# The rotary tables of a local-attention layer, scaled on GpSimd instead of VectorE from the second layer on

## What is computed

```python
q = l2norm(q) * qs          # qs, ksc: 64 numbers of this layer
k = l2norm(k) * ksc
q = q * cos * scale + rotate_half(q) * sin * scale
k = k * cos * inv + rotate_half(k) * sin * inv
out = local_attention(q, k, v)      # windows of 32 tokens, each sees itself and the one before
return out.transpose(0, 2, 1, 3).reshape(b, n, INNER) @ Wo
```

## Time and profile before

| | |
|---|---|
| median of 3 runs | 4389.28 us (4378.42 to 4394.66) |
| the profiled execution, its own time | 4373.36 us |
| span of the profiled execution | 4371.3 us |
| PE busy | 4046.5 us (93%) |
| DVE busy | 3383.3 us (77%) |
| POOL busy | 2912.9 us (67%) |
| ACT busy | 2584.3 us (59%) |
| products of `factors`, DVE L1143 | 48 instructions, 56.3 us |

### The profile page before, as it was taken

How to read it: one execution, slowest core, us unless ns; L and a number is a source line. 1 busy time by engine, 2 the same in 40 slices (tenths; PEclk the granted TensorE clock), 3 DMA queues, 4 the chain that set the end, 5 groups by cost and what they waited for, 6 DMA issues and landing times. The chain is left out here.

```text
span 4371.3 us, 151568 instructions
## 1 busy us (share of the span) xinstructions
PE 4046.5 (93%) x66856; PEld 2974.8 (68%) x66856; DVE 3383.3 (77%) x4037; ACT 2584.3 (59%) x3022; POOL 2912.9 (67%) x3425
## 2 busy tenths in 40 slices
PE   8989969999999999999868887799999999999997
PEld 5655557777877777877633333677777877777775
DVE  5636568888888888888568884788888888887884
ACT  4424436666666666666437774466666666666664
POOL 2202168887888888888534440788878888888883
PEclk9999989999999999999969997899999999999998
DMA  4304233333233232232100000323332233333221
GB/s 149 123 10 152 94 92 81 86 83 82 70 81 87 81 81 81 73 89 76 32 11 1 1 1 2 107 77 86 81 81 81 73 91 82 81 83 82 74 67 36
DMA packets 164542, 316.94 MB, mean 73 GB/s; under 512 B 38760, under 2 KB 42480, under 8 KB 156848
## 3 DMA queue, kind: packets, MB, share of 16 engines
q1 hardware_dynamic: 153520, 241.18, 20.5%
q0 software_dynamic: 10368, 66.06, 4.7%
HBM read 92.03 MB, written 20.05 MB: 26 GB/s over the span
## 5 line engine op out<-in xcount | busy, mean ns | idle before, releaser
L678 PE MATMUL psum<-loc_w_hl,loc_z_lo 128*128 128x512 f32 x1152 | 514.9, 447 | 33.1 <-DMA loc_w_hl<-parted 26.2
L1079 POOL TENSOR_TENSOR loc_prob<-loc_prob,loc_recip 128x1024 f32<-128x1024 f32 x192 | 365.6, 1904 | 183.0 <-DVE loc_recip L1201 181.6
L924 ACT ACTIVATE loc_sq<-psum 128x1024 f32<-128x1024 f32 x192 | 196.6, 1024 | 468.5 <-PE psum L680 463.5
L1061 POOL TENSOR_TENSOR loc_rc_k<-loc_rc_k,loc_rs_k 128x1024 f32<-128x1024 f32 x192 | 454.0, 2365 | 22.2 <-DVE loc_rs_k L1178 22.2
L1164 DVE TENSOR_REDUCE loc_ssq<-loc_sq 128x16 f32<-128x1024 f32 x384 | 463.8, 1208 | 3.7 <-POOL loc_rn L1057 3.6
L679 PE MATMUL psum<-loc_w_hl,loc_z_hi 128*128 128x512 f32 x1152 | 460.9, 400 | 2.2 <-issue 2.2
L680 PE MATMUL psum<-loc_w_hl,loc_z_hi 128*128 128x512 f32 x1152 | 460.5, 400 | 0.7 <-issue 0.7
L1061 POOL TENSOR_TENSOR loc_rc_q<-loc_rc_q,loc_rs_q 128x1024 f32<-128x1024 f32 x192 | 459.5, 2393 | 0.0
L775 PE MATMUL psum<-loc_PT,loc_V 64*64 64x32 f32 x24576 | 408.8, 221 | 17.5 <-issue 16.8
L775 PEld LDWEIGHTS psum<-loc_PT,loc_V 64*64 64x64 f32 x24576 | 384.9, 136 | 43.4 <-issue 19.9
L795 PEld LDWEIGHTS psum<-loc_outT,loc_wo 128*128 128x128 f32 x3072 | 378.1, 194 | 19.1 <-issue 2.5
(11 more groups left out here) (198 smaller groups left out, 9716.6 us busy)
## 6 DMA issues: line engine op xcount, KB each, us to landing
loc_V<-loc_V SPq DMA_DIRECT2D x1152, 128.0 KB
loc_V<-loc_V SPq DMA_DIRECT2D x672, 64.0 KB
loc_w_hl<-parted POOLq DMA_DIRECT2D x36, 1024.0 KB, 8.2
parted<-moe_halves POOLq DMA_DIRECT2D x18, 1024.0 KB, 5.2
moe_spread<-moe_gates SPq DMA_DIRECT2D x64, 256.0 KB, 4.1
moe_raw<-in_wqkv POOLq DMA_DIRECT2D x18, 512.0 KB, 5.9
moe_w<-in_moe_w SPq DMA_DIRECT2D x32, 256.0 KB, 3.2
loc_wo<-in_wo SPq DMA_DIRECT2D x12, 512.0 KB, 4.1
```

The source lines that it names most:

```text
L678: pe.matmul(M.bank[bank + g], z_lo[:, r, tokens], w_hl[:, k, 0, cols], start=True, stop=False)
L1061: pool.tensor_tensor(rc, rc, rs[:, :], ALU.add).then_inc(added, 1)
L1079: pool.tensor_tensor(both, both, spread_heads(recip[:, :], 2 * WINDOW), ALU.mult).then_inc(p_ready, 1)
```

## The change

DVE makes the four products of `factors` only for the first layer of each local transformer, in the order 2, 3, 0, 1. For layers 2 to 6 POOL makes them: the keys' pair at the end of step 15 of the layer before, after POOL's last addition of rotated keys, and the queries' pair in step 0, after the last queries of the layer before are scaled. DVE waits for the keys' pair ahead of its first product of keys, and for the queries' pair ahead of its first product of queries. Nothing else is moved.

```diff
@@ POOL
+            def factors(L, first):
+                if first == 2:
+                    pool.wait_ge(scales_loaded, L * 16 + 16)
+                for a in range(first, first + 2):
+                    pool.tensor_tensor(rot[:, a, :, :], M.tables[:, a, :, :],
+                                       scales[:, a, :].rearrange("p (o d) -> p o d", o=1).broadcast_to([P, TILES, DH]),
+                                       ALU.mult).then_inc(tables_ready, 1)
...
                     scaled(L, n - 1, q_added, tq_full, rc_q[:, :], 0, qk_q, q_ready)
+                if n == 0 and 0 < L < DEPTH:
+                    factors(L, 0)
...
                     total_of(L, n, k_rotated, rc_k[:, n % 2, :], rs_k, k_added)
+                if n == TS - 1 and L + 1 < DEPTH:
+                    factors(L + 1, 2)
@@ DVE
-            def factors(L):
+            def factors():
-                dve.wait_ge(scales_loaded, L * 16 + 16)
-                for a in range(4):
+                dve.wait_ge(scales_loaded, 16)
+                for a in (2, 3, 0, 1):
...
-                dve.wait_ge(tables_ready, L * 4 + 4)
...
+                    if n == 0 and L == 0:
+                        factors()
                     if n == 0:
-                        factors(L)
+                        dve.wait_ge(tables_ready, L * 4 + 2)
                     by_cosine(L, n, 2, k_squared, X_, rc_k[:, n % 2, :], k_ready, 2)
...
+                    if n == 0:
+                        dve.wait_ge(tables_ready, L * 4 + 4)
                     by_cosine(L, n, 0, q_squared, W_, rc_q[:, :], q_ready, 1)
```

## The result

Seven runs of the changed kernel gave a median of 4359.8 us (4348.68 to 4365.65), seven of the kernel before 4392.15 us (4378.4 to 4399.66). The ratio is 0.9935, with a 95% interval of 0.9913 to 0.9958: 0.65% faster, 28 us, where 10.6 us and "no change that can be told" had been forecast. The direction was right, and so was one of the two terms; the size was not. The time stands at the lower edge of the stated range, 4360 us: 4359.8 us as measured, 4360.8 us when the ratio is applied to the 4389.28 us from which the forecast was made. The profiled execution of the changed kernel took 4365.65 us. The profiled one of before, 4373.36 us, was faster than any of its seven runs, so the two spans differ by 8 us only.

The account below looks back on a forecast made before the run. The prediction took PE to be the bound nearly everywhere, with DVE holding it up only at L808. Terms of -7.2 and -3.4 us made -10.6 us, from 4389.3 to 4378.7 us; range 4360 to 4400 us.

Parts of the forecast that it names:

- The waits at L808: Term one: PE's waits for DVE at L808, over ten layer boundaries of both local transformers, vanish: -7.2 us.
- The low clock behind them: Term two: two stretches at 1.2 GHz behind the waits of 2.48 and 3.0 us at L808 vanish: -3.4 us.
- The queries' pair in POOL's idle time: POOL makes the queries' pair in its wait ahead of `normalise`, 7.24 us before and 3.48 us after: cost nothing.
- The load of the queries' weights: Keys' pair delays this load on POOL by 1.46 us against 1.48 us of slack at the tightest boundary: cost nothing.
- PE's issue waits stay near 30 us: Expected sign: PE's "issue" waits, 31.0 us in layers 2 to 6 of the first local transformer, stay near 30 us.
- PE has no idle time at the boundary of layers 3 and 4: Argument against DVE as pace: PE busy 16.05 of 16.05 us there, from first product of tile 0 to tile 1.
- An earlier DVE has nobody to serve: At the boundary of layers 3 and 4 PE passes L808 without a wait, so freeing DVE gains nothing there.
- Two of the prediction's own signs of being wrong: Step into a new layer 3 us or more shorter where PE had no wait; PE found waiting for queries' weights.
- a third or fourth wait of this kind: Reason for the range's low end, 4360 us: other executions may hold further waits of this kind, some 18 us below 4378.7.
- Nothing is gained: Rival, chance 0.26: PE arrives last at L808 at every boundary, so the moved products free nobody: 4389.3 us.
- All of DVE's time comes back: Rival, chance 0.11: DVE is the true pace of every boundary, so 51.3 us go: 4338.0 us.
- The weights come late: Rival, chance 0.06: keys' pair delays queries' weights past 1.48 us of slack; at 4.73 us a pair, 4421 us.

## Why the prediction came out as it did

**The waits at L808, -7.2 us: right.** They went to zero in the changed kernel and in every kernel that took the keys' pair off DVE, and the two windows with the long waits are shorter by 2.4 and 2.5 us.

**The low clock behind them, -3.4 us: wrong in its place.** At both boundaries for which it was reckoned the low stretch of 3.4 us is still there, behind a wait for instructions instead of the wait at L808. The clock did recover at the three boundaries that became fast, from 0.91 to 1.00, where the prediction had counted nothing.

**The price of a product on POOL, 729 ns: right,** 728 ns.

**The queries' pair in POOL's idle time, cost nothing: not quite.** At the boundary of layers 2 and 3 it was hidden as reckoned. At the three boundaries that became fast, DVE came to it first, and its first product of queries waited for POOL, 1.0 to 1.3 us. This is DVE's timeline at the boundary of layers 3 and 4:

```profile
1362.81 1.23 DVE L1170 TENSOR_TENSOR loc_rc_q<-psum,loc_rot 128x1024 f32<-128x1024 f32 x1 [1.29 <-POOL loc_rot L1085]
```

One step on, PE waits up to 0.7 us for POOL's scaled queries. The experiments with that pair on DVE were no faster.

**The load of the queries' weights, "I put the cost at nothing": the step that failed.** I asked only whether the weights would still land in time, and they did but for 0.7 us in sum. I didn't ask what the moved load had stood in front of. In the kernel before, at three boundaries, the next 16 KB of instructions came only some 6 us behind its issue, when PE had run dry; with the load 1.2 to 2.0 us later they came in time.

That the place of the load decides is shown. At these three boundaries all thirteen traces fall into two groups. In the five kernels with the load at its old place or earlier, issued at most 10.6 us behind DVE's first product of keys of tile 15, the packet starts at 14.9 to 18.0 us, and PE waits 0.9 to 4.0 us for instructions each time. In the eight with the load 11.2 us or more behind it, the packet starts at 12.3 to 14.6 us, and no wait for instructions is over 0.5 us. Both groups hold kernels with the products on DVE and kernels without, so DVE's earliness isn't what removes these waits. How the load holds the packet up inside the DMA engines no run here shows. At the other seven boundaries the changed kernel still waits for instructions, 2.4 to 5.2 us at each.

So "PE's issue waits stay near 30 us" was true of the whole (33.2 us in the two largest rows, after the 31.0 us of the earlier trace rows) and wrong at these three boundaries. "PE has no idle time at the boundary of layers 3 and 4" overlooked the 2.32 us in the earlier trace rows, and the products did not cost DVE most there: 6.36 us for the four of L1143, against 6.69 us at the boundary of layers 2 and 3 of the second transformer, where PE did wait. "An earlier DVE has nobody to serve" was wrong as well: it serves as soon as PE is no longer late. Two of the prediction's own signs of being wrong came true: the step into the new layer took 15.7 us there instead of 21.9 us, and PE was found waiting for the queries' weights, 0.46 and 0.25 us. A third expectation missed: POOL's idle time ahead of `normalise` stayed at 2.7 to 4.1 us at three boundaries.

The worth of it is the step from 0.9978 to 0.9942, 16 us, or some 10 us from the kernel that left the products out. The intervals of either pair overlap; that the later load helps when DVE is free rests on the run with the early and the run with the late load, whose intervals don't. DVE held or free, these are 0 and -10 us with the early load, +8 and -25 us with the late one.

That the time came out at the edge of the stated range is luck. The lower end was set for "a third or fourth wait of this kind", and no such wait was found; the forecast's own range, 4368 to 4389 us, was missed.

**The rivals.** "Nothing is gained" supposed that PE's instruction waits might fall so that an early DVE frees nobody. They did fall differently, but so that it freed PE at more boundaries. "All of DVE's time comes back", 51 us, is refuted: with every product left out the gain was 16 us (7 to 25). "The weights come late" met a pair of 1.41 us and no wait for weights beyond 0.5 us.

## What to carry to other kernels

When an edit shifts a large DMA, even by 1 us, look up in the DMA view which instruction packets fall under it, and count the bound engine's "issue" waits on either side; they are part of the price. So is the low clock behind such a wait: when one wait goes and another stays just ahead of it, the clock may not come back. Where two engines arrive at a meeting point almost together, as PE and DVE do here, relieving one is worth little (10 us, or a loss) and relieving both is worth more than the sum (25 us): judge such edits in pairs, because the late load alone looked like a loss of 8 to 16 us. And for work that isn't urgent, the place in the queue matters more than the engine's rate: GpSimd takes 1.8 times as long for a product as VectorE at its best, and the kernel still gained.

## What the hardware showed that was not expected

The same 1 MB load takes 9.4 us from issue to landing where it is issued 10.5 us behind the first product of keys of tile 15, and 5.5 us where it is issued at 15.7 us. In the earlier place it follows the load of the values' weights, also 1 MB, by 4.9 us. In the run with the earlier load, issued 0.65 us behind that of the values' weights, it took 9.0 us while the other took 5.4 us. What else it shares the queues with was not taken apart.

GpSimd's products never stretched, 718 to 746 ns over forty, while VectorE's of the same shape had gone from 409 to 2578 ns. What stretches in the changed kernel is a small operation of VectorE at the place where the keys' pair now runs. At the boundary of layers 3 and 4 it took 0.17 us before and 1.17 us after:

```profile
1339.81 0.17 DVE L1169 TENSOR_SCALAR loc_ssq<-loc_ssq 128x32 f32<-128x32 f32 x1
```
```profile
1349.77 1.17 DVE L1180 TENSOR_SCALAR loc_ssq<-loc_ssq 128x32 f32<-128x32 f32 x1
```

Over the whole run its min/median/max are nearly the same in both kernels, first before, then after, so it had stretched elsewhere all along:

```profile
L1169 DVE TENSOR_SCALAR loc_ssq<-loc_ssq x192: 169/502/2041, 581.8 to 4293.4; 128x32 f32<-128x32 f32 x192
```
```profile
L1180 DVE TENSOR_SCALAR loc_ssq<-loc_ssq x191: 169/541/2044, 603.1 to 4288.8; 128x32 f32<-128x32 f32 x191
```

The Trainium skill's rule of a locked port pair ("SBUF — State Buffer", section "SBUF: two separate sides") fits the tables' products, with their two SBUF inputs. L1180 has one; the same section has operations of VectorE in a two-port performance mode take the pair too, and whether L1180 runs in it no run here shows. Its other rule, that GpSimd is about twice as slow with two inputs ("GPSIMD Engine Reference", section "Engine selection"), agrees with the measured 728 ns against 409 ns at VectorE's best; that such work therefore belongs on VectorE did not hold for this place, where VectorE stood ahead of a meeting with PE and GpSimd had idle time.
